# Attention scores of the late query blocks as three products of high and low parts, issued behind the out-projection

## What is computed

```python
q = einsum('btm,mhd->bhtd', x, wq); k = ... wk; v = ... wv     # x layer-normalised, 2 heads of 128
q = frac_rope(q) * D_HEAD ** (-0.5); k = frac_rope(k) * D_HEAD ** (-0.5)
s = einsum('bhid,bhjd->bhij', q, k)
s = s - NEG * less(i, j)                                        # causal
p = softmax(s, axis=-1)
o = einsum('bhij,bhjd->bhid', p, v)
x = x + einsum('bhid,hdm->bim', o, wo)
```

## Time and profile before

| what | value |
|---|---|
| runs (3) | 1889.47, 1890.70, 1890.83 us, median 1890.7 |
| span of the profiled execution | 1886.0 us |
| attention, eight batches | about 16 to 541 us of the span |
| one inner batch | 65.6 us |
| PE busy | 1843.9 us, 98% |
| DVE busy | 1395.0 us, 74% |
| ACT busy | 881.7 us, 47% |
| POOL busy | 589.6 us, 31% |
| granted TensorE clock | 0.999 |

### The profile page before, as it was taken

One profiled execution on the slowest core, in us unless ns is written; L12 is line 12 of the kernel. 1 busy time (PEld: TensorE's weight loads), 2 busy tenths in 40 slices (PEclk: granted clock), 3 DMA queues, 4 the chain that ended last, 5 costly groups with the idle time before them and its releaser, 6 DMA issues.

```text
span 1886.0 us, 36455 instructions
## 1 busy us (share of the span) xinstructions
PE 1843.9 (98%) x12481; PEld 1541.7 (82%) x12481; DVE 1395.0 (74%) x2679; ACT 881.7 (47%) x1717; POOL 589.6 (31%) x526
## 2 busy tenths in 40 slices
PE   8999999999999999999999999999999998999998
PEld 7888888888888888878787888788878877888887
DVE  6566566556668888777777878787878788888885
ACT  6656656665554444453333333333333332444443
POOL 5313203311332222233433333333333334522211
PEclk9999999999999999999999999999999999999999
DMA  7100000000022122120000000000000001222322
GB/s 246 43 1 0 0 0 0 0 0 0 13 54 54 29 33 32 29 62 13 13 12 12 11 11 11 11 11 11 11 11 11 12 12 20 38 62 62 65 55 58
DMA packets 230630, 53.19 MB, mean 28 GB/s; under 512 B 209696, under 2 KB 228768, under 8 KB 230176
## 3 DMA queue, kind: packets, MB, share of 16 engines
q1 hardware_dynamic: 229296, 49.53, 13.0%
q10 hardware_dynamic: 1264, 2.76, 0.4%
HBM read 18.69 MB, written 8.39 MB: 14 GB/s over the span
## 4 chain that ended last, share of the span: by engine, by line
PE 74%; DVE 9%; issue 6%; POOL 4%; SPq 2%; ACT 2%; DMA 1%; DVEq 0%; ACTq 0%; POOLq 0%
PE PS L1203 16%; PE PS L1212 9%; PE PS L322 8%; PE PS L331 7%; PE PS L861 7%; PE PS L832 6%; PE PS L850 3%; PE PS L1732 3%; PE PS L1706 3%; PE PS L1668 3%; SPq L270 2%; PE PS L1711 2%; PE PS L1721 2%; PE PS L872 2%; DVE lin_zq L1504 2%
## 5 line engine op out<-in xcount | busy, mean ns | idle before, releaser
L322 PE MATMUL PS<-ln_xh,lin_w 128*128 128x512 f32 x768 | 249.9, 394 | 9.2 <-POOL ln_xl L280 5.4
L1135 ACT ACTIVATE ff_silu<-PS 128x512 f32<-128x512 f32 x192 | 114.4, 597 | 232.9 <-PE PS L1203 204.5
L1170 DVE SCALAR_TENSOR_TENSOR ff_h<-PS,ff_silu 128x512 f32<-128x512 f32 x192 | 131.2, 684 | 107.7 <-PE PS L1203 94.1
L322 PEld LDWEIGHTS PS<-ln_xh,lin_w 128*128 128x128 f32 x768 | 144.3, 188 | 47.6 <-DVE lin_kT L1487 8.6
L568 POOL TENSOR_TENSOR qk<-qk,swapped 64x128 f32<-64x128 f32 (+2 forms) x96 | 96.9, 1009 | 240.2 <-DVE swapped L712 234.4
L1154 DVE TENSOR_TENSOR ff_h_lo<-ff_h,ff_h_hi 128x512 fp32r<-128x512 f32 x192 | 165.1, 860 | 0.4
L861 PE MATMUL PS<-probT,v_a 128*128 128x128 f32 x1152 | 153.3, 278 | 0.0
L861 PEld LDWEIGHTS PS<-probT,v_a 128*128 128x128 f32 x1152 | 139.5, 192 | 14.3 <-ACT probT L632 7.4
L322 PE MATMUL PS<-ln_xl,lin_w 128*128 128x512 f32 x384 | 150.2, 391 | 0.0
L832 PE MATMUL PS<-qk 128*128 128x512 f32 (+3 forms) x384 | 145.2, 489 | 1.0 <-POOL qk L568 0.9
L722 DVE TENSOR_REDUCE neg_max<-PS 128x1 f32<-128x256 f32 (+7 forms) x128 | 95.6, 752 | 62.3 <-PE PS L835 60.9
(11 more groups left out here) (190 smaller groups left out, 5354.2 us busy)
## 6 DMA issues: line engine op xcount, KB each, us to landing
ff_raw<-ln_xn SPq DMA_DIRECT2D x464, 32.0 KB, 2.0
ln_xl<-ln_xn SPq DMA_DIRECT2D x288, 32.0 KB, 2.0
out_x<-X SPq DMA_DIRECT2D x15, 512.0 KB, 2.9
X<-in_x SPq DMA_DIRECT2D x7, 1024.0 KB, 5.5
stage<-in_w_lin SPq DMA_DIRECT2D x1, 2048.0 KB, 8.1
stage<-in_w_gate SPq DMA_DIRECT2D x2, 768.0 KB, 7.4
stage<-in_w_up SPq DMA_DIRECT2D x2, 768.0 KB, 8.8
stage<-in_w_down SPq DMA_DIRECT2D x2, 768.0 KB, 10.2
```

Of the source, the lines that this page charges most:

```text
L322: last = nc.tensor.matmul(out, w, x, start=n == 0, stop=n == len(terms) - 1)
L1135: nc.scalar.activation(silu[:, f % NB_GU, :], PS[:, f % NB_GU, :], ACT.Silu, scale=W_SCALE).then_inc(silu_done.sem, 1)
L1170: nc.vector.scalar_tensor_tensor(h[:, f % 2, :], PS[:, NB_GU + f % NB_GU, :], W_SCALE, silu[:, f % NB_GU, :], ALU.mult, ALU.mult).then_inc ...
```

## The change

It does these things, all in attention:

- `qk` is split. The first half (512 tokens) stays in `qk_first`, the second is put into the buffer of the normalised x (`ln_xn`), which is free between the transposes at a batch's start and the normalisation of the next batch.
- There are new float32r buffers: `k_hi` and `k_lo` for all 1024 keys, `q_hi` and `q_lo` for the late 512 queries. ACT makes the high parts by `qk_high` (three copies of 128x1024, in iterations 0, 1 and 3), and POOL the low parts by three subtractions, ahead of the conversion of the feed-forward weights in batch 0.
- Scores of steps 8 to 15 (query blocks 4 to 7) are three float32r products, high by high, high by low and low by high, in place of one float32 matmul.
- On PE these scores are issued at the end of step n (behind the out-projection), not behind the transposes. On ACT, exp n + 1 for n from 6 is issued behind the evacuation of O n - 1. On DVE, low output n - 1 for n from 6 is issued ahead of the row maximum n + 2.
- The normalisations wait for the last low part. In the last batch those of the feed-forward's front move later: normalise from iteration 4 to 6, 32x32 blocks from 5 to 7, statistics from 7 to 8.
- The program's scratch for dynamic DMA is set to 1024.

```diff
--- before.py
+++ after.py
@@ -459,9 +459,14 @@
         sx = [SplitTransposed(nc, sems, f"a{half}", PS[:, 2 * half:2 * half + 2, :], ident, ln, half,
                               parts=env["norm"].parts if half == 0 else (sb("a1_xh", [P, KT, UN], F32R), sb("a1_xl", [P, KT, UN], F32R)))
               for half in range(NHALF)]
-        qk = sb("qk", [P, 2, HA, T])
-
-        wqkv_raw = qk[:].rearrange("p s h t -> p (s h t)")[:, 0:KT * (WQK + HA * DA)].rearrange("p (k n) -> p k n", k=KT)
+        LATE = HA * UT
+        qk_first = sb("qk", [P, 2, HA, UN])
+        k_hi, k_lo = sb("k_hi", [P, HA, T], F32R), sb("k_lo", [P, HA, T], F32R)
+        q_hi, q_lo = sb("q_hi", [P, HA, UN], F32R), sb("q_lo", [P, HA, UN], F32R)
+        qk = [qk_first[:],
+              env["norm"].xn[:].rearrange("p t m -> p (t m)").rearrange("p (s h t) -> p s h t", s=2, h=HA)]
+
+        wqkv_raw = qk_first[:].rearrange("p s h t -> p (s h t)")[:, 0:KT * (WQK + HA * DA)].rearrange("p (k n) -> p k n", k=KT)
         swapped = sb("swapped", [P, NHALF * 2, UN])
         V = sb("v_a", [P, TB, HA * DA])
 
@@ -491,6 +496,7 @@
         proj_ready, cos_done, swap_done = (sig(f"a_{n}", NPROJ) for n in ("proj_ready", "cos_done", "swap_done"))
         sin_done = sig("a_sin_done", 2 * NHALF)
         rotated, first_rotated = sig("a_rotated", 2 * NHALF), sig("a_first_rotated", 2)
+        qk_hi_done, qk_lo_done = sig("a_qk_hi_done", 3), sig("a_qk_lo_done", 3)
         v_ready, v_done = sig("a_v_ready", TB), sig("a_v_done", TB)
         s_ready, max_done, p_done = sig("s_ready", NS), sig("max_done", NS), sig("p_done", NS)
         inv_done = sig("inv_done", NS)
@@ -507,6 +513,9 @@
             with eng.Fori(0, NB - 2) as p:
                 turn(p + 1, False, False)
             turn(NB - 1, False, True)
+
+        qk_parts = [(1, 0, k_hi[:, :, 0:UN], k_lo[:, :, 0:UN]), (0, 1, q_hi[:], q_lo[:]),
+                    (1, 1, k_hi[:, :, UN:T], k_lo[:, :, UN:T])]
 
         def score_rows(n):
 
...
@@ -564,10 +573,13 @@
                         for some in (slice(0, P), slice(P, UN)) if half == 0 else (slice(0, UN),):
                             for h in range(HA):
                                 rows = slice(h * ROT, (h + 1) * ROT)
-                                to = qk[rows, s, h, half * UN + some.start:half * UN + some.stop]
+                                to = qk[half][rows, s, h, some]
                                 done = nc.gpsimd.tensor_tensor(to, to, swapped[rows, 2 * half + s, some], ALU.add)
                             done.then_inc((first_rotated if some.stop == P else rotated).sem, 1)
                 pool.wait_ge(rotated.sem, rotated.at(b, 2 * NHALF))
+                for part, (s, half, hi, lo) in enumerate(qk_parts):
+                    pool.wait_ge(qk_hi_done.sem, qk_hi_done.at(b, part + 1))
+                    nc.gpsimd.tensor_tensor(lo, qk[half][:, s], hi.bitcast(F32), ALU.subtract).then_inc(qk_lo_done.sem, 1)
                 if first:
                     pool.wait_ge(env["ff_loaded"], 16 * NLOAD)
                     raw = env["stage"][:, 0:NW]
...
@@ -648,6 +660,11 @@
                     last = nc.scalar.activation(swapped[to:to + HALF, 2 * half + s, :], PS[of:of + HALF, PROJ_RING[m % 4], :], ACT.Copy)
                 last.then_inc(swap_done.sem, 1)
 
+            def qk_high(b, part):
+                s, half, hi, lo = qk_parts[part]
+                act.wait_ge(rotated.sem, rotated.at(b, 2 * half + s + 1))
+                nc.scalar.activation(hi, qk[half][:, s], ACT.Copy).then_inc(qk_hi_done.sem, 1)
+
             def square(part):
                 act.wait_ge(env["ff_low"], 1)
                 act.wait_ge(env["ff_squares"], part)
@@ -667,19 +684,24 @@
                 swap_halves(b, NPROJ - 1)
                 values(b, 1)
                 for n in range(NS):
-                    if n + 1 < NS:
+                    late = n + 2 >= LATE
+                    if not late:
                         exp_step(b, n + 1)
                     evacuate_probs(b, n)
+                    if n in (0, 1, 3):
+                        qk_high(b, (n + 1) // 2)
                     if n == 0:
                         values(b, 2)
                     if n + 3 < TB:
                         values(b, n + 3)
+                    if n > 0:
+                        evacuate_out(b, n - 1)
+                    if late and n + 1 < NS:
+                        exp_step(b, n + 1)
                     if n >= NS - NHALF and not last:
                         sx[n - (NS - NHALF)].act(act, b + 1)
                     if n == NS - 3 and last:
                         following.act_high(act, 0, 0)
-                    if n > 0:
-                        evacuate_out(b, n - 1)
                     if first and n > NS - NPART:
                         square(n - (NS - NPART) - 1)
                 if first:
@@ -702,7 +724,7 @@
                 half, s, h = m // NQK, m % NQK // HA, m % HA
                 at = slice(half * UN, (half + 1) * UN)
                 dve.wait_ge(proj_ready.sem, proj_ready.at(b, m + 1))
-                nc.vector.tensor_tensor(qk[:, s, h, at], PS[:, PROJ_RING[m % 4], :], cos[:, h, at],
+                nc.vector.tensor_tensor(qk[half][:, s, h, :], PS[:, PROJ_RING[m % 4], :], cos[:, h, at],
                                         ALU.mult).then_inc(cos_done.sem, 1)
 
             def times_sin(b, k):
@@ -756,11 +778,13 @@
                 times_sin(b, NPROJ // HA - 1)
                 for n in range(NS):
                     inverse(b, n)
+                    if n + 2 >= LATE:
+                        out_low(b, n - 1)
                     if n + 2 < NS:
                         row_max(b, n + 2)
                     elif not last:
                         sx[n + 2 - NS].dve(dve, b + 1)
-                    if n >= 1:
+                    if 1 <= n < LATE - 2:
                         out_low(b, n - 1)
                     if n >= 2:
                         residual(b, n - 2)
@@ -769,12 +793,14 @@
                             dve.wait_ge(x_loaded, (b + 1) * 16)
                             ln.dve_stats(dve, b + 1, (n - 4) // 2)
                         if n in (9, 11):
+                            dve.wait_ge(qk_lo_done.sem, qk_lo_done.at(b, 3))
                             ln.dve_normalise(dve, b + 1, (n - 9) // 2)
-                    if n == 4 and last:
+                    if n == 6 and last:
+                        dve.wait_ge(qk_lo_done.sem, qk_lo_done.at(b, 3))
                         following.ln.dve_normalise(dve, 0)
-                    if n == 5 and last:
+                    if n == 7 and last:
                         following.dve_blocks(dve, 0)
-                    if n == 7 and last:
+                    if n == 8 and last:
                         following.ln.dve_stats(dve, 1)
                     if n == 9 and last:
                         following.ln.dve_normalise(dve, 1)
@@ -822,15 +848,23 @@
                 i, h = steps[n]
                 if n == 0:
                     pe.wait_ge(first_rotated.sem, first_rotated.at(b, 2))
-                elif n == HA or n == HA * UT:
-                    pe.wait_ge(rotated.sem, rotated.at(b, 2 * (i // UT + 1)))
+                elif n == HA:
+                    pe.wait_ge(rotated.sem, rotated.at(b, 2))
+                elif n == LATE:
+                    pe.wait_ge(qk_lo_done.sem, qk_lo_done.at(b, 3))
                 keys = (i + 1) * P
                 for c in range(0, keys, UN):
                     w = min(UN, keys - c)
                     diag = c + w == keys
                     bank = PS[:, 2 * (n % 2) + c // UN, :]
-                    last = nc.tensor.matmul(bank[:, 0:w], qk[:, 0, h, i * P:(i + 1) * P], qk[:, 1, h, c:c + w],
-                                            start=True, stop=not diag)
+                    if n < LATE:
+                        last = nc.tensor.matmul(bank[:, 0:w], qk_first[:, 0, h, i * P:(i + 1) * P], qk_first[:, 1, h, c:c + w],
+                                                start=True, stop=not diag)
+                    else:
+                        q = slice(i * P - UN, (i + 1) * P - UN)
+                        for k, (q_part, k_part) in enumerate(((q_hi, k_hi), (q_hi, k_lo), (q_lo, k_hi))):
+                            last = nc.tensor.matmul(bank[:, 0:w], q_part[:, h, q], k_part[:, h, c:c + w],
+                                                    start=k == 0, stop=k == 2 and not diag)
                     if diag:
                         last = nc.tensor.matmul(bank[:, w - P:w], ident_b[:], mask_b[:], start=False, stop=True)
                 last.then_inc(s_ready.sem, 1)
@@ -905,9 +939,7 @@
                     if n < 2:
                         pe.wait_ge(swap_done.sem, swap_done.at(b, NPROJ - 1 + n))
                     transpose_probs(b, n)
-                    if n + 2 == HA * UT:
-                        pe.wait_ge(v_done.sem, v_done.at(b, TB))
-                    if n + 2 < NS:
+                    if n + 2 < LATE:
```

(10 more changed lines are left out.)

## The result

The changed kernel took 1912.7 us (median of 4 runs, 1911.7 to 1913.4) against 1890.8 for the kernel before on the same chip: a ratio of 1.0120, 95% interval 1.0109 to 1.0132. That is 21.9 us slower. The forecast was 1909.5 us, 18.8 slower, in a range from 1897 to 1922. The prediction was right.

The account below looks back on a forecast made before the run. TensorE, busy for 98% of the span, was taken as the bound. Products -13.8, batch waits +23.3, first batch +6.3 and last batch +3.0 make +18.8 us on 1890.7, so 1909.5, range 1897 to 1922.

Parts of the forecast that it names:

- The products: Late scores on PE, query blocks 4 to 7: three fp32r products take shorter slots than one f32 matmul, -13.8 us.
- The third rival: Late scores: the 128-column products go at half pace, +5 us less some covered waits, 1913 to 1915; chance 0.15.
- The waits of a batch: Five places where the new order makes PE wait in each batch: 3.0 us a batch, +23.3 us in all.
- (a): Transposes of step 15: PE waits for the exponential, now behind an output evacuation, with no scores as cover; 1.3 us a batch.
- (d): Value projection 4: ACT's first high-part copy delays the evacuation that it needs; 0.4 us a batch.
- (b): Steps 6 to 13: the same evacuation and exponential chain, nearly covered by out-projection and scores; 0.05 us a batch.
- (c): Weighted values 5, in step 6: PE waits for low output 4 behind row maximum 7 on DVE; 0.85 us, about 0.15 in the last batch.
- (e): Out-projections 5 and 6: the residual follows a row maximum that waits for late scores; together 0.4 us a batch.
- second rival: Late steps: the chain through ACT outlasts its cover in every step, 1 to 2 us a batch, 1918 to 1925; chance 0.13.
- The first rival: Step 15 transposes and weighted values 5: ACT and DVE run far enough ahead, no waits there, 1886.8 us; chance 0.07.
- The first batch: Step 10 transposes: POOL's subtractions delay the weight conversion and so ACT's square, PE waits; +6.3 us.
- The last batch: Weighted values 11: later 32x32 transposes and transfers hold up low output 10 on DVE, PE waits; +3.0 us.

Follow-up runs that it names:

- mended2: Changed kernel with the old issue order, late first-batch squares and normalisations, one last-batch VectorE step later, high copies in steps 1, 3, 4 after batch one; 1878.4 us.
- exp15_first: Changed kernel with exponential 15 alone put back ahead of both evacuations in ACT's step 14; 1901.7 us, ratio 1.0053 to the kernel before.
- high_later: Changed kernel with ACT's three high-part copies in steps 1, 3, 4 instead of 0, 1, 3, except in the first batch; 1910.2 us.
- squares_late: Changed kernel with the first batch's eight ScalarE squares moved to steps 12 to 15, two in each; 1908.4 us.
- blocks_late: Changed kernel with VectorE's second transfer-waiting step of the last batch moved from step 10 to step 11; 1910.6 us.
- order_only: Kernel before with only the new issue order on PE, ACT and DVE, scores still one f32 matmul; 1907.3 us, ratio 1.0092.
- wait_probe: Kernel before with ScalarE held up by unread copies in step 11, six in the first batch and twelve in the last; 1895.4 us, ratio 1.0031.
- low4_first: Changed kernel with low output 4 put ahead of row maximum 7 on DVE; 1908.7 us, ratio 1.0099 to the kernel before.
- squares_norm_late: Changed kernel with the first batch's squares in steps 12 to 15 and its two normalisations in steps 12 and 13; 1904.4 us.

## Why the prediction was right, point by point

**The products**, -13.8 us predicted. Without any wait an inner batch takes 63.84 for 65.63, 1.79 less, which is 14.3 in eight. The slots were 0.98, 1.04, 1.20 and 1.39 for the predicted 1.05, 1.06, 1.23 and 1.40. The largest gap was the 128-column shape: 0.29 for three, under the lower bound of 0.33. By its own slots the changed kernel saves (5.60 - 4.61) x 2 = 1.98 a batch. In the order of before a late score stands behind f32 transposes and pays the step from f32 work once more: S(8) with its mask takes 1.14 us in mended2 and 1.05 in the changed kernel. The third rival (half pace) is out. The 512-column products keep 0.23, so the slots estimated by the Trainium skill's gap formula (TensorE: Matmul & The Clock Gate, Back-to-back issue gap), 0.82 to 1.30, were not reached in this trace either.

**The waits of a batch**, 3.0 us predicted, 66.88 - 63.84 = 3.04 measured (3.2 if the changed kernel's own slots are the base). Of these (a) is 1.39 by exp15_first (1.3 predicted), (d) 0.42 by high_later (0.4), and (b), (c) and (e) together are the remaining 1.23 (1.3). In the late steps the chain shows nothing but PE behind PE, so (b) is not seen and the second rival is out. The size of (c) was right as a wait and wrong as a price: 0.92 us of wait, but only 0.34 comes back when low output 4 goes ahead of row maximum 7. The prediction added up what is partly one queue of VectorE. The order alone gives the same picture: 2.52 measured, 3.0 - 0.4 = 2.6 by the terms. The first rival, that ScalarE and VectorE run far enough ahead, is out.

**The first batch.** By the terms its mark moves by 6.3 + 1.3 = 7.6 us; it moved by 9.1. T(10) came at 62.30 for the predicted 62.1. The missing 1.5 us is the step that the sum didn't have: the two rows behind the wait at low clock. T(10) took 1.34 from start to start and PV(9) 1.99, together 1.5 more than the same pieces take at the full clock.

**The last batch.** By the terms +3.0 for PV(11), 1.3 for the other waits less the products, 0.7 less for (c): 3.6. Measured: 4.0. That it is so near is luck, since two errors of opposite sign stand in it. The wait itself costs 2.2 us (68.67 in squares_late, where no low clock follows it, less 66.45 in blocks_late). It is 0.8 under the term: SP issued its 16 transfers in 10.5 us where I took 11.1, and the last landed 1.4 us later (540.92 less 539.51) where I took 2.0. The low clock behind the wait costs 1.6 (70.25 less 68.67).

**Sum.** Attention: 9.1 + 6 x 1.25 + 4.0 = 20.6 for the predicted 18.8. Then 1.3 us by medians behind it, for which the prediction had nothing. The mechanism was right in every large term. What the sum lacked was the low clock, 1.5 us in the first batch and 1.6 in the last, and the stretch behind attention.

**What stays open.** The stretch behind attention holds the same instructions in all kernels and took 1351 to 1353 us in three of them (before, order_only, wait_probe), and 1353.5 to 1357.6 in the ten others. Part of the difference has a place, one unit of the feed-forward. SP starts on the unit's transfers at the same time behind the mark, 37.5 us before (572.49) and 37.6 after (593.17). But ScalarE's copy of what landed comes 49.4 us behind the mark before and 51.0 after, and PE waits for the low part (timelines of ACT, before; then ACT and PE, after):

```profile
584.33 1.06 ACT L275 ACTIVATE ff_odd_xh<-ff_raw 128x1024 fp32r<-128x1024 f32 x1 [1.94 <-DMA ff_raw<-ln_xn]
```

```profile
606.59 1.06 ACT L275 ACTIVATE ff_odd_xh<-ff_raw 128x1024 fp32r<-128x1024 f32 x1 [3.51 <-DMA ff_raw<-ln_xn]
...
610.15 0.39 PE L1248 MATMUL PS<-ff_w_hi,ff_h_hi 128*128 128x256 f32 x1 [1.59 <-POOL ff_odd_xl L280]
```

All ten kernels with the new products have this wait, 1.1 to 1.9 us long, and none of the three others has it. These ten also have the scratch of 1024 for dynamic DMA and the other layout of buffers, and no run changes one of these alone. So why the transfers land later is not shown. Nor do the places of low clock in that stretch explain it, one to four in a trace: order_only and the changed kernel have three each, at nearly the same distances behind the mark, with 1352.2 and 1356.0 us.

## What to carry to other kernels

A TensorE that is busy all the time gains from cheaper matmuls only if every producer keeps its lead. Here 1.8 us a batch was earned, and 3.0 was paid in waits, the largest of them for an exponential that waits for the weighted values of the same step. Count, for each moved piece, the time from its last input to its first user against what PE has to do in between, and do it also at the ends of the loop, where that cover is missing: half of the loss was the one step without scores.

Work handed to a side engine (three subtractions on GpSimd) is priced by what is queued behind it. When such a wait is mended, look for the second customer of the same producer. Before two waits for one engine are added up, ask whether the first hides the second.

## What the runs showed of the hardware

The granted TensorE clock fell during or shortly behind some long waits of PE, and the first work behind them ran at its lower level of 1.2 GHz instead of 2.4. The rows have it: six transposes at 1.54 for 0.85 us, products 0.42 apart for 0.23. It costs about 1.5 us a place. Granted clock by window, changed kernel: inside the wait of 6.41 us, behind it, and behind the wait of 1.92 in the last batch, where it fell about 1 us after PE had started again:

```profile
59.00:60.00 1.00, 0.00 (x0) 0.00 (x0) 0.00 (x0) 0.17 (x1) 0.98 (x2) 0.50 0.00 0
62.00:64.00 2.00, 1.70 (x8) 1.70 (x9) 2.00 (x6) 1.34 (x5) 0.44 (x1) 0.50 0.00 0
544.00:545.00 1.00, 1.00 (x7) 1.00 (x7) 0.12 (x1) 0.43 (x2) 0.00 (x0) 0.50 0.40 66
```

Then squares_late, whose two stretches hold a wait of 3.10 and one of 1.94, and wait_probe with the wait of 2.85:

```profile
60.00:70.00 10.00, 7.25 (x45) 6.72 (x46) 5.82 (x16) 2.96 (x9) 2.30 (x3) 0.83 0.01 2
535.00:545.00 10.00, 8.06 (x61) 7.16 (x60) 4.92 (x11) 4.41 (x11) 0.00 (x0) 1.00 0.23 34
```

```profile
525.00:535.00 10.00, 7.76 (x47) 5.69 (x48) 3.43 (x8) 7.55 (x17) 0.33 (x1) 1.00 0.31 45
```

With waits of 6.4 to 7.5 us it fell before the wait had ended, in all six traces that have one, and it fell behind the one of 3.10. Behind the wait of 1.92 to 1.95 us in the last batch it fell in three traces (after, exp15_first, high_later) and not in three others (low4_first, squares_late, squares_norm_late), with the same work on both sides. Behind the 2.85 us of wait_probe it did not. So a wait of two or three microseconds may or may not be paid twice, from one kernel to the next with nothing changed near it. That is the likeliest reason, though only argued, why the medians of blocks_late fell by less than its trace: 0.001 of the mean granted clock is some 4 us at the lower level, an estimate from a span of 1909 us, so its longer runs had 4 to 8 us more of it. A sum should carry it as a chance and not as a term.
